# Results of expert blocks added in memory by indirect stores, odd blocks through a second array

## The reference

```python
scores = softmax(xt @ Wg.T)                  # 16 experts in 4 groups
gidx = top_k(group maxima, 2)                # the two best groups
topi = top_k(masked scores, 4)               # four experts of each token
combine[t, topi] = scores[t, topi]
h = silu(xt @ W1[e].T) * (xt @ W3[e].T)      # 176 wide
y = sum over e of combine[t, e] * (h @ W2[e].T)
z = silu(xt @ Ws1.T) * (xt @ Ws3.T) @ Ws2.T  # the shared expert
out = x + y + z
```

## Time and profile before

| what | value |
|---|---|
| runs | 635.74, 637.88, 640.84 us; median 637.88 us |
| profiled execution | span of 630.6 us from the first to the last instruction; the page gives no other time for it |
| mean granted TensorE clock | 0.961 of full speed |
| busy | PE 567.4, DVE 394.2, ACT 249.9, POOL 196.6 us |
| blocks' stores (L1646) | 47, from 512.7 to 610.0 us |
| loads of the parts | 8 x 512 KB, median 7.1 us from issue to landing |
| stores of the output | 4 x 256 KB, median 3.6 us from issue to landing |
| expert rows in | 47 x 129 KB, median 2.2 to 2.4 us from issue to landing |

### The profile page before, as it was taken

The page is one execution under the profiler, slowest core; times in us unless marked ns, Lnnn a source line. Parts: engine busy times, 40 slices in busy tenths (PEclk is TensorE's granted clock), DMA queues, the critical chain, the costliest instruction groups (busy, mean ns, idle before and its releaser), DMA issues.

```text
span 630.6 us, 10511 instructions
## 1 busy us (share of the span) xinstructions
PE 567.4 (90%) x3751; PEld 468.2 (74%) x3751; DVE 394.2 (63%) x923; ACT 249.9 (40%) x515; POOL 196.6 (31%) x169
## 2 busy tenths in 40 slices
PE   6879998999999979999989989898899889999950
PEld 5669887898888979566566757565688777999940
DVE  3565756627454565976486465788777589655527
ACT  1325635536464534001122121044524568666630
POOL 4614441003000010422152413413617724444440
PEclk9779999999999989999999999899989999999985
DMA  8999914005030022999200000050106394344318
GB/s 233 264 221 220 230 41 167 0 2 183 2 126 2 1 98 78 346 317 331 78 1 1 0 2 1 0 223 35 68 13 247 105 309 143 107 113 124 114 22 312
DMA packets 25121, 76.93 MB, mean 122 GB/s; under 512 B 4839, under 2 KB 11631, under 8 KB 24432
## 3 DMA queue, kind: packets, MB, share of 16 engines
q1 hardware_dynamic: 19264, 62.33, 33.5%
q0 software_dynamic: 3792, 8.43, 3.8%
q10 hardware_dynamic: 2016, 5.50, 2.8%
HBM read 66.77 MB, written 28.48 MB: 151 GB/s over the span
## 4 chain that ended last, share of the span: by engine, by line
PE 58%; DVE 17%; issue 9%; DMA 7%; POOL 6%; ACT 2%; SPq 1%; POOLq 0%; DVEq 0%; ACTq 0%
PE psum L690 8%; PE psum L559 7%; PE psum L708 6%; PE psum L859 5%; PE psum L624 5%; DMA sclB<-in_scl 5%; PE psum L611 5%; PE psum L572 4%; DVE tt L1260 3%; POOL rows_of_experts L1640 3%; PE psum L752 2%; PE psum L603 2%; DVE EW L1468 2%; PE psum L590 1%; PE psum L675 1%
## 5 line engine op out<-in xcount | busy, mean ns | idle before, releaser
L1260 DVE TENSOR_TENSOR tt<-psum,tab 128x512 f32<-128x512 f32 x96 | 60.8, 682 | 33.7 <-PE psum L690 33.1
L1612 POOL TENSOR_TENSOR rp<-tt,tt 128x512 f32<-128x512 f32 x24 | 30.7, 1278 | 109.0 <-DVE tt L1260 109.0
L559 PE MATMUL psum<-xTh,W 128*128 128x512 f32 x128 | 54.9, 429 | 9.3 <-DVE W L1160 7.4
L708 PE MATMUL psum<-rp,Mb 128*128 128x512 f32 x128 | 57.8, 597 | 0.3 <-DVE rp L1285 0.3
L859 PE MATMUL psum<-EW,xgh 128*128 x188 | 56.7, 344 | 0.5 <-issue 0.4
L1646 POOL DMA_INDIRECT parts_of_tokens<-yb,xg x39 | 40.4, 1035 | 51.4 <-ACT yb L1093 51.1
L1230 DVE TENSOR_TENSOR OTl<-psum,OTh 128x512 fp32r<-128x512 f32 x32 | 22.1, 691 | 54.3 <-ACT OTh L960 54.3
L559 PE MATMUL psum<-xTl,W 128*128 128x512 f32 x128 | 53.6, 418 | 0.0
L993 ACT ACTIVATE qP<-psum 128x512 f32<-128x512 f32 x16 | 9.6, 598 | 96.0 <-PE psum L708 96.0
L690 PE MATMUL psum<-xTh,Ah 128*128 128x512 f32 x96 | 42.3, 441 | 4.4 <-DVE ex_la L1340 2.3
L708 PEld LDWEIGHTS psum<-rp,Mb 128*128 128x128 f32 x128 | 24.0, 192 | 26.4 <-issue 25.6
(11 more groups left out here) (254 smaller groups left out, 1530.7 us busy)
## 6 DMA issues: line engine op xcount, KB each, us to landing
rows_of_experts<-in_empty SPq DMA_DIRECT2D x8, 2064.0 KB, 32.0
exr<-in_ex SPq DMA_DIRECT2D x9, 608.0 KB, 6.4
xg<-rows_of_experts SPq DMA_DIRECT2D x39, 129.0 KB, 2.2
exr<-in_ex ACTq DMA_DIRECT2D x7, 608.0 KB, 5.0
raw<-in_codes SPq DMA_DIRECT2D x4, 1024.0 KB, 20.4
sclB<-in_scl SPq DMA_DIRECT2D x16, 256.0 KB, 12.1
yv<-parts_of_tokens SPq DMA_DIRECT2D x8, 512.0 KB, 7.1
raw<-in_codes SPq DMA_DIRECT2D x4, 512.0 KB, 17.3
```

The costliest lines, as they stand in the source:

```text
L559: mm = pe.matmul(ap, W[:, kt, m, 512 * hq + 128 * h:512 * hq + 128 * h + 128], xp[:, kt, 512 * g:512 * g + 512], start=(n == 0), stop=(n = ...
L708: mm = pe.matmul(ap, Mb[:, 4 * hp + 2 * kk + half_, :], rp[(j0 + kk) % 3][:, half_, :], start=(n == 0), stop=(n == 3))
L1260: return tt_(b3(tt[n][:, :], 64), b3(src, 64), tab[:, j % 3, n, :].unsqueeze(1).to_broadcast([128, 8, 64]), ALU.mult)
L1612: tt_(o[:, 0, :], tt[0][:, :], tt[1][:, :], ALU.subtract).then_inc(s_rp_lo, 1)
```

## The change

The results of blocks are no longer stored as parts and added at the end. POOL's indirect store adds them (`compute_op=ALU.add`) to a row of memory: even blocks to the output itself, odd blocks to a second array, `sums_of_odd_blocks`, of 1024 + 128 rows. The result row of a copy is now the row of its token, the same for all four. Padding rows get one of 128 rows behind the tokens, and are stored like the others. The output has these 128 rows too and is cut on the host.

An addition reads and writes its row, so two blocks that may hold the same token must not be under way at once: POOL's store of block b waits until that of b - 2, to the same array, has landed, and the first one until the output holds `xs`. `xs` with the shared expert added is stored to the output by SP in `add_shared(t)` of odd t, two tiles at a time, when DVE has done both. `clear` has two DMAs more, for the odd array and the output's last 128 rows, and scatters wait for eleven clearing DMAs, not nine. At the end POOL waits for the last two stores and issues one DMA that adds the odd array to the output. `finish` on DVE and SP is gone, with the tiles `yv`. ACT's reuse of `yb` and SP's of `xg` wait for the same blocks as before, by the new semaphores.

```diff
+        def added(b):
+            return d_sum[b % 2], 16 * (b // 2 + 1)
 ...
             def block_down(b):          # ACT
                 sc_.wait_ge(*ps.filled("by", b))
                 if b >= 4:
-                    sc_.wait_ge(d_yb[(b - 4) % NX], 16 * ((b - 4) // NX + 1))
+                    sc_.wait_ge(*added(b - 4))
 ...
-            def finish():               # DVE
-                for t in range(NT):
-                    ve.wait_ge(*ps.emptied("y", t))
-                    ve.wait_ge(d_yv[t], 16)
-                    tt_(yv[t][:, 0:2, :], yv[t][:, 0:2, :], yv[t][:, 2:4, :], ALU.add).then_inc(s_sum4, 1)
-                    ve.wait_ge(s_sum4, 2 * t + 1)
-                    tt_(xs[:, t, :], yv[t][:, 0, :], xs[:, t, :], ALU.add).then_inc(s_sum4, 1)
-                    ve.wait_ge(s_sum4, 2 * t + 2)
-                    tt_(xs[:, t, :], yv[t][:, 1, :], xs[:, t, :], ALU.add).then_inc(s_y, 1)
 ...
             def scatter(t, of=(0, 1, 2, 3)):
-                po.wait_ge(d_clear, 144)
+                po.wait_ge(d_clear, 176)
 ...
             def block_down(b):          # POOL
                 po.wait_ge(*ps.emptied("by", b))
                 to = bass.IndirectOffsetOnAxis(ap=xg[b % NX][:, 256:257].bitcast(i32), axis=0)
-                nc.gpsimd.indirect_dma_start(out=parts_of, out_offset=to, in_=yb[b % 4][:, :],
-                                             in_offset=None, bounds_check=4 * 1024 - 1, oob_is_err=False).then_inc(d_yb[b % NX], 16)
+                if b >= 2:
+                    po.wait_ge(*added(b - 2))
+                elif b == 0:
+                    po.wait_ge(d_out, 16 * NT // 2)
+                nc.gpsimd.indirect_dma_start(out=(out, odd_sums)[b % 2], out_offset=to, in_=yb[b % 4][:, :],
+                                             in_offset=None, bounds_check=TOKENS - 1, oob_is_err=True,
+                                             compute_op=ALU.add).then_inc(d_sum[b % 2], 16)
+
+            def finish():               # POOL
+                po.wait_ge(*added(NB - 2))
+                po.wait_ge(*added(NB - 1))
+                nc.gpsimd.dma_start(out[0:1024, :].rearrange("(p t) c -> p (t c)", t=8),
+                                    odd_sums[0:1024, :].rearrange("(p t) c -> p (t c)", t=8),
+                                    accum_op=ALU.add, max_dma_last_dim=4096).then_inc(d_merge, 16)
+                po.wait_ge(d_merge, 16)
 ...
             def clear(k):               # SP
-                    dma(rows_of[2048 * k:2048 * k + 128, :], empty[:, 0:ROW]).then_inc(d_clear, 16)
+                    rows = empty.rearrange("p (j c) -> (p j) c", c=ROW)
+                    dma(rows_of[2048 * k:2048 * k + 128, :], rows[0:128, :]).then_inc(d_clear, 16)
+                    dma(odd_sums, rows[0:TOKENS, 0:256]).then_inc(d_clear, 16)
+                    dma(out[1024:TOKENS, :], rows[0:128, 0:256]).then_inc(d_clear, 16)
 ...
             def fetch(b):               # SP
                 if b >= NX:
-                    sp.wait_ge(d_yb[b % NX], 16 * (b // NX))
+                    sp.wait_ge(*added(b - NX))
 ...
-            def finish():               # SP
-                for i in range(NX):
-                    sp.wait_ge(d_yb[i], 16 * ((NB - 1 - i) // NX + 1))
-                for t in range(NT):
-                    dma(yv[t][:, :, :], parts_of[512 * t:512 * t + 512, :].rearrange("(p k) c -> p k c", k=4)
-                        ).then_inc(d_yv[t], 16)
-                for t in range(0, NT, 2):
-                    sp.wait_ge(s_y, t + 2)
-                    dma(out[:, t:t + 2, :], xs[:, t:t + 2, :]).then_inc(d_out, 16)
-                sp.wait_ge(d_out, 16 * NT // 2)
+            def add_shared(t):          # SP
+                if t % 2 == 1:
+                    sp.wait_ge(*ps.emptied("y", t - 1))
+                    sp.wait_ge(*ps.emptied("y", t))
+                    dma(out[0:1024, :].rearrange("(p t) c -> p t c", t=8)[:, t - 1:t + 1, :],
+                        xs[:, t - 1:t + 1, :]).then_inc(d_out, 16)
 ...
-    token = 128 * np.arange(8)[None, :, None] + p[:, None, None]
-    plan[:, 173:205] = (4 * token + np.arange(4)).reshape(128, 32).astype(np.int32).view(f)
+    row = 8 * p[:, None, None] + np.arange(8)[None, :, None]
+    plan[:, 173:205] = (row + 0 * np.arange(4)).reshape(128, 32).astype(np.int32).view(f)
 ...
-    empty[:, :, 256] = np.full((128, 16), 4 * 1024, np.int32).view(f)
+    empty[:, :, 256] = (1024 + np.arange(2048) % 128).reshape(128, 16).astype(np.int32).view(f)
```

More of the change, by code:

```diff
@@ L24 @@
 SPARE = NE * CAP
+TOKENS = 1024 + 128
 ROW = 258
@@ L398, in program @@
         exr = [at(f"exr{i}", slot(EXPERT_AT[i]) + 4 * 1216, [128, 1216]) for i in range(NE)]
-        yv = [at(f"yv{t}", E0 + 4096 * t, [128, 4, 256]) for t in range(NT)]
         wo = at("wo", R2, [128, NH, 256], R)
@@ L464, in program @@
         rows_of = nc.dram_tensor("rows_of_experts", (SPARE + 128, ROW), F).ap()
-        parts_of = nc.dram_tensor("parts_of_tokens", (4 * 1024, 256), F).ap()
+        odd_sums = nc.dram_tensor("sums_of_odd_blocks", (TOKENS, 256), F).ap()
         tri128 = cst[:, 0:128]
@@ L484, in program @@
         d_xg = [sem(f"block{i}_in") for i in range(NX)]
-        d_yb = [sem(f"parts{i}_out") for i in range(NX)]
-        d_yv = [sem(f"parts_in{t}") for t in range(NT)]
+        d_sum, d_merge = [sem("even_block_added"), sem("odd_block_added")], sem("sums_merged")
         d_out = sem("stored")
@@ L505, in program @@
         s_bsl, s_bx_hi, s_bt_hi, s_one = (sem(n) for n in ("bsilu", "bx_hi", "bt_hi", "one"))
-        s_sum4 = sem("sum4")
-        s_sl, s_sl2, s_gt_hi, s_y = sem("silu"), sem("silu2"), sem("gt_hi"), sem("y")
+        s_sl, s_sl2, s_gt_hi = sem("silu"), sem("silu2"), sem("gt_hi")
         def wqk(hq, h):
@@ L1528, in vector_program @@
                     "add_shared": add_shared, "block_turn": block_turn,
-                    "block_hidden": block_hidden, "block_back": block_back, "finish": finish}
+                    "block_hidden": block_hidden, "block_back": block_back}
             for name, *where in ORDER:
@@ L1761, in sync_program @@
                     "query_weights": query_weights, "load13": load13, "clear": clear, "load2": load2, "expert_in": expert_in,
-                    "fetch": fetch, "finish": finish}
+                    "fetch": fetch, "add_shared": add_shared}
             for name, *where in ORDER:
@@ L1884 @@
         aps[name] = nc.dram_tensor(f"in_{name}", a.shape, _mybir.dt.from_np(a.dtype), kind="ExternalInput").ap()
-    out = nc.dram_tensor("out_0", (128, 8, 256), _mybir.dt.float32, kind="ExternalOutput").ap()
+    out = nc.dram_tensor("out_0", (TOKENS, 256), _mybir.dt.float32, kind="ExternalOutput").ap()
     program(nc, out=out, **aps)
@@ L1888 @@
     y = r.results[0]["out_0"]
+    y = y[0:1024].reshape(128, 8, 256)
     return _np.ascontiguousarray(y.transpose(1, 0, 2)).reshape(16, 64, 256)
```

2 lines of the change are left out of this document (1 added, 1 removed).

## The result

The changed kernel takes 655.5 us in the median of five runs (650.0 to 656.75), the kernel before 638.5 us (635.74 to 640.84) beside it: a ratio of 1.025, interval 1.0216 to 1.0285. It is slower by 17 us; 649 was forecast. A run more than 1.5% above the fastest of its kernel is left out of the ratios, which is one run in all, in experiment 8. The profiled execution took 650.0 us, with a span of 648.2, 17.6 us over the span before. It was the fastest of the five; the other four took 655.47 to 656.75.

A forecast was written before the change was run, and what follows sets the result against it. PE was taken as busy all the time from 542 to 602 us, before an 18.5 us tail. Terms +3.7 + 2.0 + 11.1 + 2.4 + 2.0 - 10.2 = +11.0 us gave 649 us, range 631 to 667.

The forecast's parts named there:

- the 7.3 us carried over: Whole kernel: the runs' median of 637.88 us lies 7.3 us above the profiled span; this was carried over unchanged.
- The law of the pace: POOL's block stores: landing plus 0.75 us per chain, two blocks a round, so 4.75 / 2 = 2.375 us a step.
- Landing of 4.0 us: POOL's adding stores: 2.8 us plain, 1.1 for reading the destination, 0.1 for descriptors; 4.0 us (2.8 to 5.5).
- The path to PE: POOL's lag beyond about 3.5 us reaches ACT four blocks on, then PE, not SP's fetches; no further delay.
- Thirty steps: Middle block stores, 545 to 605 us: 2.375 instead of 2.006 us a step, +11.1 us.
- first twelve: First block-store steps, beside the experts' loads: four blocks at about 3.5 us, partly regained; +2.0 us (0 to 4).
- last three: Last three block-store steps: 3 x 2.375 us instead of 4.76, +2.4 us.
- The tail: Behind the blocks: final loads, adds and stores (18.5 us) give way to an 8.3 us merge tail; -10.2, last landing +2.0.
- The head: Start of the blocks: SP's first fetch waits behind the early store of the last tiles, 3.7 us later.
- the chain stays hidden: Block stores: landing stays under 3.25 us, middle steps cost nothing, 634 us; hidden or nearly hidden had chance 0.29.
- Rival 2: Block stores hidden, head absorbed too, merge at the copying rate: 628 to 631 us; chance 0.16.
- The third rival: Adding stores: read and write wholly in series, landing 5.0 us, 666 us; chance 0.18.

The follow-up runs named there:

- experiment 8: Changed kernel with SP's store of the last two tiles of xs moved behind the first six fetches; ratio 1.015 to the kernel before.
- experiment 1: Changed kernel with the blocks' stores plain instead of adding, all else kept; 628.25 us against 629.75 for the kernel before, ratio 0.9984.
- experiment 2: Changed kernel with three arrays in turn, three chains and two merges; 639.42 us against 629.75 for the kernel before, ratio 1.0142.
- experiment 3: Kernel of experiment 2 with a single array, the output, each store waiting for the one before, no merge; one execution, span 737.1 us.
- experiment 9: Changed kernel again, unchanged, on the variants' chip; 646.57 us against 628.45 for the kernel before, ratio 1.0276.
- experiment 6: Kernel before plus SP's early stores of xs in pairs of tiles, to an array nothing reads, ahead of the fetches; 634.46 us against 629.75.
- experiment 7: Kernel before again, unchanged, one execution for a trace from the variants' chip; 627.09 us, span 625.8.

## Why the prediction was right

The forecast was slower, by the chain of stores, and the chain it is: without the addition the 17 us are gone (experiment 1), with three chains the pace of the middle is back (2), with one it is landing plus 0.83 us (3). 11.0 us were forecast, 17.5 measured in the first trace and 17.0 and 18.1 between medians. The time of 649 us also rests on the 7.3 us carried over from span to median. Where a run has both, its time is only 1.2 to 1.5 us above its span in the kernel before and 1.8 to 2.0 in the changed one; the rest is that the profiled executions, before and after alike, were faster than the medians. The difference hardly depends on it.

- **The law of the pace** (landing plus 0.75 us, over the number of chains) holds closely with one chain: the rows of experiment 3 give 3.73 + 0.11 + 0.72 = 4.56 (4.56 measured); plain stores, 2.4 us, have 3.26 a step, and half rows, 3.2, mostly 4.0 to 4.2. The fixed part is 0.83 to 0.86 rather than 0.75 us: to the 0.71 us of the earlier trace rows come the wait's release and a register move. With three chains, and with two and plain stores, the law gives less than 2.0 us, and PE's 2.00 to 2.01 holds. With two adding chains the slower one counts, the odd array's: its landings of 4.1 us (median, experiment 9) give (4.1 + 0.83) / 2 = 2.465, and 2.465 is measured; with the late store they are 3.9 us, which gives 2.37, and 2.41 is measured. That the forecast's 2.375 was so near the 2.40 of the first trace is partly luck: its fixed part was 0.1 us short, and it knew of one landing for both arrays, when stores to the output land in 3.8 us (median, experiment 8).
- **Landing of 4.0 us**: 3.65 to 4.34 in the first trace's chain of waits, 3.8 over both arrays in experiment 8 and 4.1 for the odd array in experiment 9; why the odd array's take longer isn't shown. Its parts were put wrongly: a plain store alone lands in 2.4 us and not 2.8, POOL's instruction is 0.58 us longer and not 0.1, and what is left of the 1.3 us between a plain and an adding store alone, 0.7, stands against 1.1 for the read; that it is the packets' longer time on the engines, 0.76 us by the queue, is argued from that match.
- **The path to PE** was put wrongly: ACT was to meet the wait four blocks on, and SP's fetches, ten blocks behind, were not to feel it. In the first trace PE waited nine times for a block's rows and ACT three times for a landing, and in experiment 9 ten times against five. It is one delay by either path, as the prediction said, so the sum isn't touched.
- **Thirty steps** +11.1 us forecast, +11.9 and +13.8 measured; first twelve +2.0, measured +2.8 and +3.1; last three +2.4, measured +1.8 and +2.2. The blocks in all: +15.5 forecast without the last landing, +16.6 and +19.4 measured.
- **The tail** -8.2 us with the last landing, -8.3 and -8.2 measured; the merge took 7.7 us from issue to landing (7.9 in experiment 9), 7.5 forecast. Its sum was put against the Trainium skill's rule (Collectives: The Full Stack, "Why ReduceScatter is half of AllGather"), which gave 8.8 us; the measured 7.7 lies between the two, and doesn't tell whether the second read or the fixed part was put too high.
- **The head** is the term that was mis-sized: 3.7 us forecast, 5.5 to 5.6 measured in four traces with the early stores ahead of the fetches (experiments 1, 2, 6, 9) against the kernel before in experiment 7, and 5.1 to 5.3 against its first trace; in 6, 4.3 until the fetch and 1.3 behind it. SP needed longer from DVE's end to the fetch than put (1.7 instead of 1.2 us), and the lower clock behind PE's idle time, 1.1 of the 1.3 us by the rows of experiments 6 and 7, had not been thought of. The first profile's 9.2 us hold 4 to 5 us more that none of the later traces has.

So of the 6 to 7 us between the forecast and the measured difference about 2 are the head's and 1 to 4 the blocks'; what is left isn't told apart from the spread of runs.

**The rivals.** That the chain stays hidden needed a landing under 3.25 us; it was 3.8 to 4.1. Experiment 1 shows how near it was: plain stores, 2.4 us alone, are hidden in the mean. Rival 2 needed the head absorbed as well, and it wasn't. The third rival's landing of 5.0 us is refuted, by at most 4.34 in the first trace's chain and 3.7 alone in experiment 3; whether reading and writing go in series within that isn't told. What stays open: the 2 to 3 us of experiment 8 that its trace doesn't have, the slower first twelve steps with three arrays, the odd array's longer landings, and what ended ACT's wait of 7.4 us in the first profile.

## What to carry to other kernels

A store that adds in memory puts a full landing, and the start of the instruction behind the wait, between two stores to one array: before building it, hold (landing + 0.85 us) / arrays against the present pace, and take the landing of an adding store (3.7 us for 128 rows of 1 KB here), not of a plain one (2.4). With two arrays in turn the slower chain sets the pace, here with landings of 4.1 us. A third array frees the pace, but each array costs a merge, 7.7 to 8.0 us for 1 MB here. A wait put ahead of fetches on a queue that goes in order cost its own length here, 4.3 us, and then 1.1 us of lower clock, as PE had nothing else to do; the last store put six fetches later gave 3.5 us back.

## What was not expected of the hardware

- Without the addition, the stores kept a mean step of 2.003 us though 14 of 36 started only when a landing released them: the mean decides, not the single wait.
- An adding store makes 144 packets for 128 rows, against 48 of a plain one, and the queue's time of the DMA engines triples at the same bytes, from 5.7 to 17.9 us over 16 engines. Half the bytes per row took 0.5 us from the landing, and nothing from POOL's 1.55 us.
- Behind a stretch of six microseconds in which PE was busy for 1.4, the granted clock was 0.50 in the next six, though PE was busy in 5.7 of them; the first six matmuls of the experts took 2.12 us for 1.24.
